# The second VectorE pass of an expert unit one gap later, alternating unit buffers, and a chunk loop written out

## The chip, the cores and the metric

One core of one Trainium2 chip. The metric is the device time of the whole launch in microseconds; smaller is better. TensorE does the matmuls, VectorE, ScalarE and GpSimd work on tiles in SBUF and (the first two) in PSUM, SyncE issues most transfers. Each engine runs its own list of instructions in order; they meet at semaphores.

## The reference

Input x of 32 sequences of 64 tokens of 128 features goes through four blocks, each added to its input:

```
x = x + recurrent_attention(layernorm(x), cond, ctx)   # 64 steps, one after the other
x = x + moe(layernorm(x))                              # 64 experts of width 64, top 8, plus a shared one
x = x + transformer_block(layernorm(x), cond, ctx)     # two attentions and a gated feed-forward
x = x + x @ weight.T + pooled(x) @ disha
```

The change touches the first two. A step of the recurrence computes logits = [x, h] @ W_attn.T + b, their softmax, the weighted sum over the context, comb = relu([x, applied] @ W_comb.T + b) and h = tanh(comb @ W_ih.T + h @ W_hh.T + b). The mixture of experts computes, for each expert, silu(x @ Wg) * (x @ Wu) * coef and multiplies it by Wd; all are summed.

## The kernel before

**Tiling.** The 64 steps of the recurrence are cut into 4 chunks (CH) of 16 steps (SPC). A chunk has 512 tokens (CT), which are the 512 columns of its tiles. As soon as a chunk has left the recurrence, its experts are computed, beside the recurrence of the next chunks. The experts go in pairs: 32 pairs (PAIRS) and the shared expert are 33 units (UNITS), numbered 0 to 32; unit 32 is the shared one.

**Stages and gaps.** All engines walk through the same plan, `stages` (line 455). Stage k runs the recurrence of chunk k, the norm, routing and first units of chunk m = k-1, and the last units of chunk k-2 (`tail`). Stages 0 and 1 are written out, stages 2 and 3 are a hardware loop (`Fori`, line 459), stages 4 and 5 have no recurrence. A stage has 64 gaps, four for each step of the recurrence (IDLE_GAPS); the place of a gap is its number modulo 4. The text calls four gaps of one step "a step", and counts them from 0 to 15 in a stage. In a gap an engine first does its operation of the recurrence and then what else the plan puts there. The order of the work on each engine is thus written by hand, and no engine goes past a wait.

**The recurrence by places** (function `rnn` of each engine). Place 0: TensorE makes the logits (lines 1451, 1452, 1462), VectorE the negative maximum `nmax` (1020), ScalarE the exp (765). Place 1: VectorE the reciprocal (1024) and `diag` (1026), TensorE eT (1465), VectorE `eb` in two parts (1030, 1034). Place 2: TensorE the 49 matmuls of comb (1469, 1475), VectorE `comb` (1038). Place 3: TensorE hn (1483, 1484), ScalarE the tanh `Hc` (771).

**A unit** n of chunk m, which begins at gap g = 28 + 2n of stage m+1 (units from gap 64 on run in the next stage, as `tail`):

- TensorE, gap g: six matmuls into PSUM bank n % 2 and bank 2 + n % 2 (line 1529).
- ScalarE, gap g: tanh into `th` (801). For n = 0 it copies the routing weights `coefT` before (796); SyncE stores them and loads them back, broadcast, as `coef_wide` (524, 533).
- VectorE, gap g+1: the first pass, `ga` = (th + 1) * bank (1168), and at once the second, `gu` = ga * other bank (1173).
- GpSimd, gap g+1: `hid` = gu * coef (637).
- TensorE, gap g+5: the down matmul into bank 5, over all units (1536).

So in gaps of odd number VectorE has both passes, and before them the operations of place 1 or 3. The buffers `th`, `gu`, `hid` and the banks are indexed by n % 2. As 33 is odd, unit 32 of a chunk and unit 0 of the next have the same buffers; `others` (line 448) gives the count up to which the users of a buffer must have come, and for n = 0 it is the whole chunk before. Units 31 and 32 both begin at gap 90, 26 of the next stage. Their sum is added to the residual by `add_units` (1175 to 1180) at gap END_GAP = 96, gap 32 of the next stage; the down matmul of unit 0 of the next chunk, which overwrites bank 5, waits for it (x2_ready, line 1534).

In the profile the tiles ga, gu and hid are named ex, th is thcb, coef_wide is xn, and PSUM is ps.

Of the kernel before, what the change touches and what calls it, by code (L numbers as in the profile page):

```python
# [8 lines left out]
ALU = mybir.AluOpType  # L9
ACT = mybir.ActivationFunctionType  # L10
# [6 lines left out]
WSCALE = 16.0  # L17
# [33 lines left out]
def build(nc, ins, out):  # L51
# [5 lines left out]
    CH = 4  # L57
# [3 lines left out]
    PAIRS = E // 2  # L61
# [11 lines left out]
    with ctx:  # L73
# [40 lines left out]
        wg = sb("wg", [P, PAIRS, 2, P], F16)  # L114
        wu = sb("wu", [P, PAIRS, 2, P], F16)
        wd = sb("wd", [P, PAIRS, P])
        swgu = sb("swgu", [P, 2, 2, P], F16)
        swd = sb("swd", [P, P])
# [81 lines left out]
        th = thcb[:, 0]  # L200
        ctx_tok = thcb[:, :, :, :].rearrange("p a b (n d) -> p (a b n) d", d=P)
        ga = ex[:, 2, :]
        gu = ex[:, 3:5, :]
        hid = ex[:, 5:7, :]
# [104 lines left out]
        def bank(i):  # L309
            return ps[:, i, :]  # L310
# [6 lines left out]
        def first(k):  # L317

            return isinstance(k, int) and k == 0
# [117 lines left out]
               **{gap: ("route", i) for i, gap in enumerate(g for g in range(10, 26) if g % IDLE_GAPS)}, 26: "coefT"}  # L437
        UNITS = PAIRS + 1
        U0 = 28
        unit_gap = [U0 + 2 * min(n, PAIRS - 1) for n in range(UNITS)]  # L440
        END_GAP = unit_gap[-1] + 6

        def units_at(gap, m, tail, delay=0):

            return [(chunk, n) for chunk, g in ((tail, gap + GAPS), (m, gap)) if chunk is not None
                    for n in range(UNITS) if unit_gap[n] + delay == g]

        def others(m, n):

            if isinstance(m, int) and m == 0 and n < 2:  # L450
                return None

            return m * UNITS + n - (1 if n else 0)

        def stages(eng, stage):

            stage(0, None, None, True)
            stage(1, 0, None, True)
            with eng.Fori(0, CH - 2) as j:
                stage(j + 2, j + 1, j, True)  # L460
            stage(CH, CH - 1, CH - 2, False)
            stage(CH + 1, None, CH - 1, False)

# [92 lines left out]
        def _(pool):  # L556
# [71 lines left out]
            def unit(m, n):  # L628
                done = m * UNITS + n
                pool.wait_ge(s["gu_ready"], done + 1)  # L630
                if n < PAIRS:
                    pool.wait_ge(s[f"coef_in{n // 2 % 2}"], 32 * (m * (PAIRS // 4) + n // 4 + 1))
                if others(m, n) is not None:
                    pool.wait_ge(s["y_ready"], others(m, n))
                wide = coef_wide[:, n // 2 % 2, n % 2 * CT:(n % 2 + 1) * CT]
                other = wide if n < PAIRS else k_shared.broadcast_to([P, CT])
                nc.gpsimd.tensor_tensor(hid[:, n % 2, :], gu[:, n % 2, :], other, ALU.mult)\  # L637
                  .then_inc(s["hid_ready"], 1)

            def stage(k, m, tail, recur):  # L640
# [66 lines left out]
            for n in range(ITEMS):  # L707
                k, g, a, j = item(n)
# [10 lines left out]
            with pool.Fori(0, CH // 2) as j:  # L719
                k = Tally(pool, s["f_pool"], 4)  # L720
# [11 lines left out]
        def _(act):  # L732
# [58 lines left out]
            def unit(m, n):  # L791
                if n == 0:
                    act.wait_ge(s["coefT_ps"], m + 1)
                    if not first(m):
                        act.wait_ge(s["coef_stored"], 16 * m)
                    nc.scalar.copy(coefT, bank(7)[0:E, :]).then_inc(s["coefT_ready"], 1)
                done = m * UNITS + n
                act.wait_ge(s["gu_ps"], done + 1)
                if others(m, n) is not None:
                    act.wait_ge(s["gu_ready"], others(m, n))  # L800
                nc.scalar.activation(th[:, n % 2, :], bank(n % 2), ACT.Tanh, scale=0.5 / WSCALE)\  # L801
                  .then_inc(s["th_ready"], 1)

            def stage(k, m, tail, recur):
# [84 lines left out]
            for n in range(-1, ITEMS + 1):  # L889
                k, j = divmod(n, 4)  # L890
# [39 lines left out]
        def _(dve):  # L930
            V = nc.vector
# [83 lines left out]
            def rnn(k, st, place):  # L1015
                t = k * SPC + st
                logits_bank, comb_bank, eT_bank, _ = (bank(i) for i in step_banks(k))
                if place == 0:
                    dve.wait_ge(s["logits_ready"], t + 1)
                    V.tensor_reduce(nmax[:, :], logits_bank[0:B, 0:L], AX_X, ALU.max, negate=True)\  # L1020
                     .then_inc(s["nmax_ready"], 1)
                elif place == 1:
                    dve.wait_ge(s["exp_ready"], t + 1)
                    rt.settle(V.reciprocal(rsum[:, :], esum[:, :]))

                    V.tensor_scalar(diag[:, :], ident[0:B, 0:B], rsum[:, :], 2.0, mul, mul)\  # L1026
                     .then_inc(s["diag_ready"], 1)
                    dve.wait_ge(s["eT_ready"], t + 1)

                    V.tensor_tensor(eb[:, 0, :], eT_bank[:, ET], ebmask[:, :], mul).then_inc(s["eb_hi"], 1)  # L1030
                    dve.wait_ge(s["eb_hi"], t + 1)
                    for a in range(2):
                        r = slice(a * L, (a + 1) * L)
                        V.tensor_tensor(eb[r, 1, a::2], eT_bank[r, ET][:, a::2], eb[r, 0, a::2], sub)\
                         .then_inc(s["eb_lo"], 1)
                elif place == 2:
                    dve.wait_ge(s["comb_ps_ready"], t + 1)
                    V.tensor_scalar(comb[:, :], comb_bank[:, COMB], bcomb[:, :], 0.0, add, ALU.max)\
                     .then_inc(s["comb_ready"], 1)
# [120 lines left out]
                                    csum[:, :].unsqueeze(2).unsqueeze(3).broadcast_to([P, TPC, PAIRS, 2]), mul)\  # L1160
                     .then_inc(s["coef_ready"], 1)

            def unit(m, n):
                done = m * UNITS + n
                dve.wait_ge(s["th_ready"], done + 1)
                if others(m, n) is not None or n == 1:
                    dve.wait_ge(s["gu_ready"], done)
                V.scalar_tensor_tensor(ga[:, :], th[:, n % 2, :], 1.0, bank(n % 2), add, mul)\  # L1168
                 .then_inc(s["unit_dve"], 1)
                dve.wait_ge(s["unit_dve"], done + 1)  # L1170
                if others(m, n) is not None:
                    dve.wait_ge(s["hid_ready"], others(m, n))
                V.tensor_tensor(gu[:, n % 2, :], ga[:, :], bank(2 + n % 2), mul).then_inc(s["gu_ready"], 1)  # L1173

            def add_units(m):
                dve.wait_ge(s["y_ready"], (m + 1) * UNITS)
# [5 lines left out]
            def stage(k, m, tail, recur):  # L1182
                if recur:
                    rt.round(k)
                if m is not None:
                    pt.round(m)
                for gap in gaps_of(m, tail):
                    st, place = divmod(gap, IDLE_GAPS)
                    if recur:
                        rnn(k, st, place)  # L1190
                    if first(k) and gap in SPLITS:
                        c = SPLITS[gap]
                        dve.wait_ge(s["weights_hi"], c + 1)
                        V.scalar_tensor_tensor(halves_of[c][1], landing_view(c), WSCALE, halves_of[c][0], mul, sub)\
                         .then_inc(s["weights_lo"], 1)
                    if first(k) and gap in LATE_OUT and setup_sem[LATE_OUT[gap]] == "setup_dve":
                        setup(LATE_OUT[gap])
                    if first(k) and gap in STOPS:
                        stops(STOPS[gap])
                    if m is not None and gap in PRO:  # L1200
                        part(m, PRO[gap])
                    if tail is not None and gap + GAPS == END_GAP:
                        add_units(tail)
                    for chunk, n in units_at(gap, m, tail, 1):
                        unit(chunk, n)

            stages(dve, stage)

# [200 lines left out]
        def _(pe):  # L1409
# [109 lines left out]
            def unit(m, n):  # L1519
                if n == 0:  # L1520
                    pe.wait_ge(s["xn2T_ready"], 2 * m + 2)
                    pe.wait_ge(s["weights_lo"], WEIGHTS)
                    pe.wait_ge(s["moe_w_in"], 16 * MOE_DMAS)
                if others(m, n) is not None:
                    pe.wait_ge(s["gu_ready"], others(m, n))
                for w, bk in ((wg, n % 2), (wu, 2 + n % 2)):
                    of = w[:, n] if n < PAIRS else swgu[:, bk // 2]
                    for i, (u, v) in enumerate(HALVES):
                        last = mm(bank(bk), of[:, u, :], xn2_half(m, v), start=(i == 0), stop=(i == 2))  # L1529
                last.then_inc(s["gu_ps"], 1)  # L1530

            def down(m, n):
                if n == 0 and not first(m):
                    pe.wait_ge(s["x2_ready"], m)
                pe.wait_ge(s["hid_ready"], m * UNITS + n + 1)
                mm(bank(5), wd[:, n, :] if n < PAIRS else swd[:, :], hid[:, n % 2, :],  # L1536
                   start=(n == 0), stop=(n == UNITS - 1)).then_inc(s["y_ready"], 1)

            def stage(k, m, tail, recur):
# [215 lines left out]
```

## Time and profile before

| | us |
|---|---|
| median of 3 runs | 1224.45 |
| lowest and highest | 1223.15, 1224.51 |
| profiled execution | 1223.28 |
| its span, first to last instruction | 1221.2 |
| TensorE matmuls busy | 1055.8 (86%) |
| VectorE busy | 742.1 (61%) |
| GpSimd busy | 512.8 (42%) |
| ScalarE busy | 429.8 (35%) |
| mean granted clock of TensorE | 0.864 of 2.4 GHz |

A timeline has one line for an instruction, or for a few alike: its start in us from the span's start, its time in us, the engine (PE is TensorE, PEld its weight loads, DVE VectorE, ACT ScalarE, POOL GpSimd), the line of the kernel, what it writes and reads, how many, and in brackets the idle time of the engine before it with what ended it. The time of an instruction includes what it waits for once it has started. The clock is 1.00 for 2.4 GHz and 0.50 for 1.2 GHz.

### The profile page before, as it was taken

To read this page: it belongs to the slowest core of one execution; us is meant where nothing else is said; L and a number is where in the kernel's file an instruction comes from. 1 tells how busy PE (TensorE), PEld (TensorE's weight loads), DVE (VectorE), ACT (ScalarE), POOL (GpSimd) and SP (SyncE) were. 2 spreads that over 40 slices of the span, in tenths; PEclk is the share of its full clock that TensorE was granted. 3 is DMA by queue.
4 is the path that set the end of the run, shared out by engine and by line. 5 is a ranking of instruction groups with operands and counts; after the bars stand their busy time and mean duration, and the time that the engine had idled before them with its cause. 6 is when DMAs were issued, how large, how long until landed. Compare 5 with 4: busy or idle time off the path is not lost. (4 is left out here: it accounts for less than half of the span.)

```text
span 1221.2 us, 31046 instructions
## 1 busy us (share of the span) xinstructions
PE 1055.8 (86%) x12668; PEld 701.2 (57%) x12668; DVE 742.1 (61%) x1882; ACT 429.8 (35%) x798; POOL 512.8 (42%) x452
## 2 busy tenths in 40 slices
PE   2699777789998999989997997799899999997867
PEld 2577655545555555545553443677677677775445
DVE  5544444445567554765569565678777678775553
ACT  1211011112221221212221222677778677775111
POOL 4788200003322332322333455576666666664010
PEclk9555555559999998889999999799999999999878
DMA  9020026012212221113222342000000000000000
GB/s 241 19 57 1 1 43 121 1 47 63 70 53 54 74 70 54 53 36 74 70 70 70 90 121 70 1 3 3 3 3 2 3 3 3 2 3 3 1 18 17
DMA packets 46066, 51.67 MB, mean 42 GB/s; under 512 B 22086, under 2 KB 36584, under 8 KB 45928
## 3 DMA queue, kind: packets, MB, share of 16 engines
q1 hardware_dynamic: 43010, 48.71, 15.7%
q8 instruction: 101, 1.65, 0.6%
q10 hardware_dynamic: 2918, 1.01, 0.5%
q14 instruction: 37, 0.30, 0.1%
HBM read 48.13 MB, written 1.57 MB: 41 GB/s over the span
## 5 line engine op out<-in xcount | busy, mean ns | idle before, releaser
L637 POOL TENSOR_TENSOR ex<-ex,xn 128x512 f32<-128x512 f32 x128 | 162.5, 1271 | 368.0 <-DVE ex L1173 275.3
L801 ACT ACTIVATE thcb<-ps 128x512 f32<-128x512 f32 x132 | 78.6, 596 | 283.1 <-PE ps L1529 283.1
L702 POOL TENSOR_TENSOR wu<-encC,wu 128x1024 f16<-128x1024 f32 x64 | 137.7, 2167 | 56.5 <-ACT encC L876 56.5
L1168 DVE SCALAR_TENSOR_TENSOR ex<-thcb,ps 128x512 f32<-128x512 f32 x132 | 90.6, 687 | 89.8 <-ACT thcb L801 87.1
L1536 PE MATMUL ps<-ex,wd 128*128 128x512 f32 x256 | 138.9, 625 | 1.9 <-POOL ex L637 1.9
L1529 PE MATMUL ps<-xnT,wg 128*128 (+1 forms) x384 | 109.3, 395 | 6.5 <-DVE ex L1173 6.4
L1529 PE MATMUL ps<-xnT,wu 128*128 (+1 forms) x384 | 109.7, 396 | 0.0
L1589 PE MATMUL ps<-wg,M 128*128 128x128 f16 x1536 | 98.2, 222 | 2.1 <-DVE wg L1262 2.1
L1589 PEld LDWEIGHTS ps<-wg,M 128*128 128x128 f16 x1536 | 93.1, 99 | 6.8 <-DVE wg L1262 2.5
L1173 DVE TENSOR_TENSOR ex<-ex,ps 128x512 f32<-128x512 f32 x132 | 90.7, 687 | 7.3 <-POOL ex L637 2.8
L696 POOL TENSOR_TENSOR wd<-wd,a_sum 128x512 f32<-128x512 f32 x64 | 66.5, 1042 | 65.7 <-DVE a_sum L1293 65.7
L1624 PE MATMUL ps<-N,wg 128*128 128x512 f16 x384 | 91.9, 381 | 0.6 <-DVE ex L1275 0.5
L869 ACT CAST wu<-ps 128x1024 f16<-128x1024 f32 x64 | 65.0, 1015 | 75.7 <-PE ps L1624 75.7
L1475 PEld LDWEIGHTS ps<-eb,encC 128*128 128x128 f16 x3072 | 91.1, 101 | 0.0
L1475 PE MATMUL ps<-eb,encC 128*128 128x2 f16 x3072 | 88.6, 164 | 0.0
L1284 DVE TENSOR_REDUCE a_max<-ps 128x8 bf16<-128x512 f32 x64 | 44.3, 692 | 48.6 <-PE ps L1604 48.3
L765 ACT ACTIVATE e_sb<-ps,nmax 32x128 f32<-32x128 f32 x64 | 22.9, 358 | 132.8 <-DVE nmax L1020 132.8
L1465 PE MATMUL ps<-diag,e_sb 32*128 32x32 f32 x128 | 31.2, 327 | 43.8 <-DVE diag L1026 43.8
L1529 PEld LDWEIGHTS ps<-xnT,wu 128*128 128x128 f16 x384 | 38.8, 101 | 49.3 <-issue 6.9
L876 ACT COPY encC<-ps 128x1024 f32<-128x1024 f32 x64 | 64.8, 1012 | 5.4
L1465 PEld LDWEIGHTS ps<-diag,e_sb 32*128 32x128 f32 x128 | 23.7, 229 | 71.7 <-DVE diag L1026 68.1
L1529 PEld LDWEIGHTS ps<-xnT,wg 128*128 128x128 f16 x384 | 31.4, 99 | 58.1 <-issue 30.2
(295 smaller groups left out, 1937.1 us busy)
## 6 DMA issues: line engine op xcount, KB each, us to landing
xn<-coef_rows SPq DMA_DIRECT2D x128, 256.0 KB, 3.8
thcb<-in_L_ffn_Wg SPq DMA_DIRECT2D x8, 256.0 KB, 3.8
thcb<-in_L_ffn_Wu SPq DMA_DIRECT2D x8, 256.0 KB, 3.1
wd<-in_L_ffn_Wd SPq DMA_DIRECT2D x2, 1024.0 KB, 11.4
xtok<-in_x SPq DMA_DIRECT2D x4, 256.0 KB, 6.0
thcb<-in_ctx SPq DMA_DIRECT2D x2, 512.0 KB, 11.1
wu<-in_L_xcond_attn_wq SPq DMA_DIRECT2D x2, 512.0 KB, 10.9
wu<-in_L_xcond_attn_wk SPq DMA_DIRECT2D x2, 512.0 KB, 10.6
```

The source lines that it names most:

```text
L637: nc.gpsimd.tensor_tensor(hid[:, n % 2, :], gu[:, n % 2, :], other, ALU.mult)\
L696: nc.gpsimd.tensor_tensor(half, half, a_sum[:, u, :].rearrange("p (m b) -> p m b", b=2).unsqueeze(3) .broadcast_to([P, 4, 2, 64]), ALU.mul ...
L702: nc.gpsimd.tensor_tensor(z[:, 1, 8 * u:8 * u + 8, :], a_Zc[:, u], z[:, 0, 8 * u:8 * u + 8, :], ALU.subtract)\
L801: nc.scalar.activation(th[:, n % 2, :], bank(n % 2), ACT.Tanh, scale=0.5 / WSCALE)\
L869: nc.scalar.copy(a_Z[:, n % 2, 0, 8 * u:8 * u + 8, :], ps[:, 2 * u:2 * u + 2, :].rearrange("p v (h d) -> p (v h) d", d=P)).then_inc(s["a_Z ...
L1168: V.scalar_tensor_tensor(ga[:, :], th[:, n % 2, :], 1.0, bank(n % 2), add, mul)\
L1173: V.tensor_tensor(gu[:, n % 2, :], ga[:, :], bank(2 + n % 2), mul).then_inc(s["gu_ready"], 1)
L1475: last = mm(comb_ps[:, 2 * j:2 * j + 2], encC[:, u, j, :], eb[:, v, 2 * j:2 * j + 2], start=False, stop=(v == 1 and j == NPAIR - 1))
L1529: last = mm(bank(bk), of[:, u, :], xn2_half(m, v), start=(i == 0), stop=(i == 2))
L1536: mm(bank(5), wd[:, n, :] if n < PAIRS else swd[:, :], hid[:, n % 2, :], start=(n == 0), stop=(n == UNITS - 1)).then_inc(s["y_ready"], 1)
L1589: m = mm(bank(b)[:, h * P:(h + 1) * P], M[a][:, u, 4 * b + h, :], a_h[:, k % 2, v, j * P:(j + 1) * P], start=(i == 0), stop=(i == 2))
L1624: m = mm(bank(2 * u + v), src[:, x, :], N[a][:, w, h:h + 4, :].rearrange("p h d -> p (h d)"), start=(i == 0), stop=(i == 2))
```

## The change

Three things. First, VectorE's `unit` is split: `gated` (first pass) stays in gap g+1, `product` (second pass) goes to gap g+2, right behind VectorE's operation of the recurrence in that gap, which for g+2 is that of place 0 or 2. Second, unit 32 begins at gap 91 in place of 90, END_GAP becomes 97, and `th`, `gu`, `hid` and the banks alternate by the running number of the unit over all chunks (`side`), so that each unit has other buffers than the one before; `others` is then the same formula for all units. Third, the hardware loop over stages 2 and 3 is written out.

```diff
-        unit_gap = [U0 + 2 * min(n, PAIRS - 1) for n in range(UNITS)]
+        unit_gap = [U0 + 2 * n - (n == PAIRS) for n in range(UNITS)]
         END_GAP = unit_gap[-1] + 6
...
-            if isinstance(m, int) and m == 0 and n < 2:
-                return None
-
-            return m * UNITS + n - (1 if n else 0)
+            done = m * UNITS + n
+            return done - 1 if done >= 2 else None
+
+        def side(m, n):
+
+            return (m * UNITS + n) % 2
...
-            with eng.Fori(0, CH - 2) as j:
-                stage(j + 2, j + 1, j, True)
+            for k in range(2, CH):
+                stage(k, k - 1, k - 2, True)
...
-            def unit(m, n):
+            def gated(m, n):
                 done = m * UNITS + n
                 dve.wait_ge(s["th_ready"], done + 1)
-                if others(m, n) is not None or n == 1:
+                if done:
                     dve.wait_ge(s["gu_ready"], done)
-                V.scalar_tensor_tensor(ga[:, :], th[:, n % 2, :], 1.0, bank(n % 2), add, mul)\
+                V.scalar_tensor_tensor(ga[:, :], th[:, side(m, n), :], 1.0, bank(side(m, n)), add, mul)\
                  .then_inc(s["unit_dve"], 1)
+
+            def product(m, n):
+                done = m * UNITS + n
                 dve.wait_ge(s["unit_dve"], done + 1)
                 if others(m, n) is not None:
                     dve.wait_ge(s["hid_ready"], others(m, n))
-                V.tensor_tensor(gu[:, n % 2, :], ga[:, :], bank(2 + n % 2), mul).then_inc(s["gu_ready"], 1)
+                V.tensor_tensor(gu[:, side(m, n), :], ga[:, :], bank(2 + side(m, n)), mul).then_inc(s["gu_ready"], 1)
...
                     if recur:
                         rnn(k, st, place)
+                    for chunk, n in units_at(gap, m, tail, 2):
+                        product(chunk, n)
...
                     for chunk, n in units_at(gap, m, tail, 1):
-                        unit(chunk, n)
+                        gated(chunk, n)
```

The other lines of the diff put `side(m, n)` in the place of `n % 2` on GpSimd, ScalarE and TensorE.

## Rows read from the trace of the kernel before

**Rows 1.** The page: its head, and TensorE's granted clock in 40 slices.

```profile
span 1221.2 us, 31046 instructions
...
PEclk9555555559999998889999999799999999999878
```

**Rows 2.** Windows: stretch, its length, busy us (instructions) of each engine, clock, DMA.

```profile
449.03:456.77 7.74, 7.74 (x79) 4.35 (x78) 4.13 (x11) 1.82 (x7) 2.53 (x2) 1.00 0.24 70
332.49:343.86 11.37, 11.21 (x95) 6.62 (x94) 5.87 (x20) 2.33 (x8) 2.10 (x2) 1.00 0.17 48
472.24:489.53 17.29, 15.67 (x95) 9.01 (x94) 6.07 (x21) 2.44 (x8) 2.29 (x2) 0.70 0.12 33
```

**Rows 3.** Timeline of a steady step: start, us, engine, line, out<-in [idle before].

```profile
449.88 0.69 DVE L1173 TENSOR_TENSOR ex<-ex,ps 128x512 f32<-128x512 f32 x1
...
450.64 1.27 POOL L637 TENSOR_TENSOR ex<-ex,xn 128x512 f32<-128x512 f32 x1 [2.42 <-DVE ex L1173]
...
450.83 0.21 DVE L1020 TENSOR_REDUCE nmax<-ps 32x1 f32<-32x64 f32 x1 [0.27 <-PE ps L1462]
...
451.39 0.81 PE L1529 MATMUL ps<-xnT,wu 128*128 x3
451.56 0.15 DVE L1024 RECIPROCAL rsum<-esum 32x1 f32<-32x1 f32 x1 [0.52 <-ACT e_sb L765]
451.75 0.23 DVE L1026 TENSOR_SCALAR diag<-ident,rsum 32x32 f32<-32x32 f32 x1
...
452.13 0.29 PEld L1465 LDWEIGHTS ps<-diag,e_sb 32*128 32x128 f32 x2 [0.42 <-DVE diag L1026]
```

**Rows 4.** Line 1026 in 280 to 330 and in 580 to 622: ns least/median/most.

```profile
L1026 DVE TENSOR_SCALAR diag<-ident,rsum x7: 228/228/230, 281.1 to 327.5; 32x32 f32<-32x32 f32 x7
...
L1026 DVE TENSOR_SCALAR diag<-ident,rsum x6: 228/228/231, 581.6 to 620.3; 32x32 f32<-32x32 f32 x6
```

**Rows 5.** Timeline of a step that is late on VectorE.

```profile
364.11 0.69 DVE L1173 TENSOR_TENSOR ex<-ex,ps 128x512 f32<-128x512 f32 x1
...
364.71 0.20 DVE L1020 TENSOR_REDUCE nmax<-ps 32x1 f32<-32x64 f32 x1
...
365.62 0.55 DVE L1026 TENSOR_SCALAR diag<-ident,rsum 32x32 f32<-32x32 f32 x1
...
366.22 0.40 PE L1465 MATMUL ps<-diag,e_sb 32*128 32x32 f32 x2 [1.24 <-DVE diag L1026]
```

**Rows 6.** Timeline at 82.9 and at 92.4, VectorE and GpSimd starting together.

```profile
82.95 1.30 DVE L1026 TENSOR_SCALAR diag<-ident,rsum 32x32 f32<-32x32 f32 x1
82.96 1.26 POOL L618 TENSOR_TENSOR cen<-xn,ex 128x512 f32 x1 [0.19 <-POOL ex L616]
...
92.45 0.23 DVE L1026 TENSOR_SCALAR diag<-ident,rsum 32x32 f32<-32x32 f32 x1
92.53 1.28 POOL L616 TENSOR_TENSOR ex<-ex 128x512 f32<-128x512 f32 x1 [0.19 <-POOL ex L616]
```

**Rows 7.** Timeline of gaps 32 and 33 of stage 2.

```profile
410.86 2.49 POOL L637 TENSOR_TENSOR ex<-ex,xn 128x512 f32<-128x512 f32 x2 [4.63 <-DMA xn<-coef_rows]
410.89 0.21 DVE L1020 TENSOR_REDUCE nmax<-ps 32x1 f32<-32x64 f32 x1 [1.13 <-PE ps L1462]
411.08 1.22 DVE L1179 TENSOR_TENSOR xT<-xT,ps 128x512 f32 x1
...
413.44 0.40 PE L1465 MATMUL ps<-diag,e_sb 32*128 32x32 f32 x2 [1.18 <-DVE diag L1026]
```

**Rows 8.** The loop's line on TensorE's queue, and the first logits behind it.

```profile
L459 PEldq COMPARE_BRANCH  x2: 83/1802/3521, 470.8 to 623.9; - x2
...
474.63 0.40 PE L1451 MATMUL ps<-w_attnT,xnc 128*32 128x128 f32 x2 [1.62 <-issue]
```

**Rows 9.** Timeline: three matmuls of a unit at the lower clock.

```profile
482.98 1.49 PE L1529 MATMUL ps<-xnT,wu 128*128 x3
```

**Rows 10.** Timeline: the last down of the last chunk.

```profile
755.24 1.13 PE L1536 MATMUL ps<-ex,swd 128*128 128x512 f32 x2
```

More of the change, by code:

```diff
@@ L636, in unit @@
                 other = wide if n < PAIRS else k_shared.broadcast_to([P, CT])
-                nc.gpsimd.tensor_tensor(hid[:, n % 2, :], gu[:, n % 2, :], other, ALU.mult)\
+                nc.gpsimd.tensor_tensor(hid[:, side(m, n), :], gu[:, side(m, n), :], other, ALU.mult)\
                   .then_inc(s["hid_ready"], 1)
@@ L800, in unit @@
                     act.wait_ge(s["gu_ready"], others(m, n))
-                nc.scalar.activation(th[:, n % 2, :], bank(n % 2), ACT.Tanh, scale=0.5 / WSCALE)\
+                nc.scalar.activation(th[:, side(m, n), :], bank(side(m, n)), ACT.Tanh, scale=0.5 / WSCALE)\
                   .then_inc(s["th_ready"], 1)
@@ L1525, in unit @@
                     pe.wait_ge(s["gu_ready"], others(m, n))
-                for w, bk in ((wg, n % 2), (wu, 2 + n % 2)):
+                for w, bk in ((wg, side(m, n)), (wu, 2 + side(m, n))):
                     of = w[:, n] if n < PAIRS else swgu[:, bk // 2]
@@ L1535, in down @@
                 pe.wait_ge(s["hid_ready"], m * UNITS + n + 1)
-                mm(bank(5), wd[:, n, :] if n < PAIRS else swd[:, :], hid[:, n % 2, :],
+                mm(bank(5), wd[:, n, :] if n < PAIRS else swd[:, :], hid[:, side(m, n), :],
                    start=(n == 0), stop=(n == UNITS - 1)).then_inc(s["y_ready"], 1)
```

## The prediction

> **What bounds the kernel now.** I read the page first, for the span of 1221.2 us [rows 1]. The run it comes from took 1223.28 us, so 2.1 us lie around the span; the median of the three runs shown is 1224.45. All sums below start from 1223.28. The change touches only the part from the first unit (step 7 of stage 1) to the last `add_units`, about 262 to 757 us. Then I cut this part into steps of four gaps, which a tanh of the recurrence (line 771) marks. A step that has two units and nothing else takes 7.74 us, with TensorE busy all 7.74 [rows 2]. So TensorE, in order, is the bound there, and whatever makes it wait adds in full.
>
> Where could it be made to wait? Within the step the recurrence is a chain: logits, maximum (line 1020), exp, reciprocal (1024), diag (1026), eT on TensorE (1465). TensorE covers the chain with one unit's six matmuls [rows 3]. The reader should see two things. `product` (line 1173) ends at 450.57, but the maximum waits for TensorE's logits until 450.83: in such a step the second pass delays the maximum by nothing, and its old place is empty time. And diag ends at 451.98, with TensorE at eT from 452.13: that chain has 0.1 us to spare. Steps like this one, with diag at 0.23 us and eT about 0.15 behind it, are 24 in all: 7 in stage 1, 8 in stage 2, 9 in stage 3 [rows 4] (the first seven and the last six).
>
> Ten further steps, early in stages 2 and 3, are late on VectorE, which has routing work: there the maximum does come behind `product`, and TensorE stands still before eT, 1.24 us in the one shown [rows 5]; these pauses run from 0.2 to 1.9 us.
>
> **The port.** diag takes 0.23 us alone. Where GpSimd runs it takes 0.55 and ends at 366.17 [rows 5], while the GpSimd operation started right behind `product`, at 0.07 after its end. Two pairs show who wins [rows 6]. At 82.95 diag starts 0.01 us before a GpSimd operation, yet lasts 1.30 and ends 0.03 behind it. At 92.45 GpSimd starts 0.08 us behind it and diag takes 0.23. So diag loses unless it leads by more than 0.01, and surely wins from 0.08 on; when it loses it waits to GpSimd's end plus 0.03.
>
> **Part 1, the second pass behind the recurrence's operation.** For even gaps of place 0, `product` now stands between the maximum and the reciprocal. Worked out on the steady step [rows 3], with the maximum unchanged at 450.83: the next operation of VectorE starts 0.19 later (410.89 to 411.08) [rows 7], so `product` runs 451.02 to 451.71. GpSimd's multiply starts 0.07 to 0.08 behind it (450.57 to 450.64) [rows 3], at 451.79, and ends 1.27 later, 453.06. The reciprocal can start 0.09 before `product` ends (364.80 to 364.71) [rows 5], at 451.62, which is behind exp's 451.56; diag 0.19 later, at 451.81. GpSimd is first by 0.02, where it has been seen to win even 0.01 late. So diag ends at 453.09 and eT starts 0.05 later (366.17 to 366.22) [rows 5]: 453.14 in place of 452.13, **+1.01 us** per step. Bounds: +0.0 if diag gets in first (it would end at 452.04, within TensorE's own time), and +1.1 if the 0.1 spare is not there. TensorE has nothing to put in the gap, as its queue is in order. 24 steps: **+24.2**. Step 7 of stage 2, where eT had 0.35 behind diag: +0.8. There, TensorE's unit 0 also has to wait for `product` of unit 31, now behind the maximum in the same gap (line 1525's wait), for 0.9 us; this falls into the same pause and costs nothing more while diag stalls.
>
> Late steps: the maximum comes up to 0.72 earlier, since the pass no longer precedes it, but diag then ends 2.25 behind the maximum (0.19 + 0.69 + 0.07 + 1.27 + 0.03) in place of 1.46. Six steps, whose logits are ready over 0.72 before: +0.08 each. Four, whose maximum is late by 0.03 to 0.21 only: +0.5 to +0.74, together 2.7. Sum **+3.1**.
>
> At place 2 `product` goes behind comb (line 1038). comb feeds hn, which stands behind six matmuls on TensorE: nobody waits, only two pauses of 0.22 could go. Taken as 0. The consumers have room: down(n) comes five gaps behind unit n, and unit n+2 four.
>
> The Trainium skill, page SBUF — State Buffer, section SBUF: two separate sides, calls the pair of ports that VectorE and GpSimd share an exclusive lock: whichever starts first has it for the whole instruction. By its letter diag should have won at 82.95; there it lost, so I go by the rows [rows 6]. It speaks against this change just the same: with GpSimd 0.02 us first, it gives +1.0 too, and with diag first the rival below.
>
> **Part 2, unit 32 in gap 27, END_GAP 97.** `add_units` moves to gap 33, where down(0) waits for it. In step 8 of stages 2 and 3, before: maximum, add of 1.22, diag behind two GpSimd operations, pause of 1.18, eT at 413.44 [rows 7]. After: diag slips in behind the first GpSimd operation (eT about 412.2), then eb (1.0), add (1.2), and only then down(0), about 414.6 in place of 413.8: +0.8 each, up to 2.0 if diag has to wait for both. I take 0.8, since the diag that waited at 82.95 ended 0.03 behind one GpSimd operation, though more were queued [rows 6]: **+1.6**. Without the recurrence, unit 32 stands behind one more down, 1.0 to 1.1 us [rows 10]: the copy of coefT in stage 4, on which the loads depend that bind there, comes 1.1 later, and the very end about 0.8 later: **+1.9**. The alternating buffers take away the wait of unit 0 for unit 32, worth 0.1 in stage 2 and nothing in stage 4, where those loads bind.
>
> **Part 3, the loop written out.** TensorE's branch back takes 3.52 us, and TensorE is idle 1.62 us before the logits [rows 8]. The step takes 17.29 us at a clock of 0.70, the same step of stage 2 11.37 at 1.00 [rows 2]. Without the branch I take all of it, **-5.9**; the other end is -1.4, the idle time alone, if the clock falls anyway. Code in a straight line was fetched unseen everywhere else, so its length costs 0. The row only says "issue"; that a taken branch forces a fetch of its target is what the Trainium skill says (Runtime: NRT & Kernel Launch, section Instruction fetch mechanics).
>
> **The clock.** Of nine pauses of TensorE over 1 us in stages 2 and 3, four were followed by a stretch at 1.2 GHz in place of 2.4; the page shows it as 8 in slices 16 to 18 (458 to 550 us) [rows 1]. Three matmuls take 1.49 there against 0.81 [rows 3, 9], so a unit costs 1.3 more. The change makes 25 new pauses of about 1 us and lengthens four. They are shorter than the ones that did it, so I take a quarter: 6 or 7 falls by 1.4 us, **+9**. Bounds 0 and +20 (half of them).
>
> **The sum.** 24.2 + 0.8 + 3.1 + 1.6 + 1.9 - 5.9 + 9 = +34.7, so 1223.3 + 34.7 = **1258 us**, +2.8%.
>
> **Rivals.**
> (A) The same, and the clock holds: 1249 us. For it: in stage 2 five pauses of 1.2 to 1.9 us left the clock alone. Chance 0.22.
> (B) diag wins the race, and the change is faster. Place: lines 1024 to 1026 behind `product`. It needs GpSimd 0.03 to 0.10 us later against diag than the rows say. Then the 24 steps cost 0, the six late ones gain 0.96 each (diag ends 1.21 behind a maximum 0.72 earlier), the four others 0.2 to 0.43, together -7.0; with +1.6, +1.9 and -5.9: 1214 us. Against it: all intervals used repeat to 0.01 us from step to step. Chance 0.12.
> (C) The move does not do what it says, because some steps stall and others not, or the written-out loop gives more than its idle time and clock show: 1225 to 1240. Chance 0.06.
> (D) Forecast, stalls and some half clock: 1252 to 1275. Chance 0.60.
>
> **How the numbers follow.** The likeliest case gives 1258. The range 1236 to 1273 holds D but for its top, A, and half of C: about 0.8. What a measurement can tell from no change is about 0.2%, 2.4 us. Faster is B: 0.12. Same 0.02. Slower is the rest: 0.86.
>
> **What would show it.** Right: diag (line 1026) at about 1.3 us in most steps, ending 0.03 behind line 637; a steady step of 8.75 us; TensorE idle 1.0 before line 1465; no long branch near 471 us; step 0 of stage 3 near 11.4 us. Wrong: diag at 0.23 with line 637 starting behind it, and steps of 7.74. If the clock's page row shows more than slices 16 to 18 below 9, the time goes towards 1273 or over.

## The result, and the profile after

The changed kernel takes **1279.71 us** (median of 4 runs, 1274.23 to 1282.30) against 1223.80 for the kernel before (4 runs): ratio **1.0454**, 95% interval 1.0415 to 1.0492. It is slower, as predicted, but by 56 us, not by 35, and outside the range of 1236 to 1273. The profiled execution took 1278.36 us, with a span of 1276.6.

The page of the changed kernel: its head, and TensorE's granted clock in 40 slices. It answers to [rows 1].

```profile
span 1276.6 us, 30526 instructions
...
PEclk9555555579898988988889899899999999999878
```

Before, only slices 16 to 18 of 10 to 25 stood below 9. Now nine of the slices 11 to 23 do. By windows over the whole part in question, from the end of step 7 of stage 1 to the end of the recurrence (stretch, length, busy us (instructions) of TensorE, its weight loads, VectorE, ScalarE and GpSimd, clock, DMA share, GB/s), first the kernel before, then the changed one:

```profile
268.95:625.27 356.32, 341.18 (x3215) 192.06 (x3216) 208.88 (x620) 78.72 (x211) 107.30 (x87) 0.95 0.23 62
```

```profile
269.19:677.58 408.39, 371.58 (x3215) 206.54 (x3216) 232.72 (x621) 81.16 (x211) 106.91 (x87) 0.88 0.20 54
```

This pair splits the loss in two. The stretch is 52.1 us longer. The same 3215 matmuls are busy for 30.4 us more (the clock, 0.88 in place of 0.95), and TensorE is idle for 21.7 us more (36.8 less 15.1). What TensorE waited for in the same stretch (sum in us, times, longest), before and after:

```profile
PE ps L1465 <- DVE diag L1026: 12.5, 12, 1.9
```

```profile
PE ps L1472 <- DVE diag L1028: 30.7, 33, 1.8
PE ps L1543 <- DVE xT L1184: 3.8, 2, 1.9
PE ps L1536 <- DVE ex L1178: 2.0, 2, 1.0
```

So diag is the wait that was turned on, 33 times in place of 12. The second line is `add_units`, behind which down(0) stands in step 8. The third is unit 0, which in step 7 of stages 2 and 3 waits for `product` of unit 31.

A steady step of the changed kernel as a timeline, which answers to [rows 3]:

```profile
289.30 0.21 DVE L1022 TENSOR_REDUCE nmax<-ps 32x1 f32<-32x64 f32 x1 [0.99 <-PE ps L1469]
289.44 0.67 DVE L1178 TENSOR_TENSOR ex<-ex,ps 128x512 f32<-128x512 f32 x1
...
290.03 0.15 DVE L1026 RECIPROCAL rsum<-esum 32x1 f32<-32x1 f32 x1
290.18 1.26 POOL L639 TENSOR_TENSOR ex<-ex,xn 128x512 f32<-128x512 f32 x1 [2.04 <-DVE ex L1178]
290.21 1.26 DVE L1028 TENSOR_SCALAR diag<-ident,rsum 32x32 f32<-32x32 f32 x1
...
291.53 0.40 PE L1472 MATMUL ps<-diag,e_sb 32*128 32x32 f32 x2 [0.87 <-DVE diag L1028]
```

GpSimd starts 0.03 us ahead of diag, diag lasts 1.26 in place of 0.23 and ends 0.03 behind GpSimd, and eT follows 0.06 later. diag ends 2.17 behind the maximum's start; the prediction had 2.25. Step 7 of stage 2 shows that not every VectorE operation is held up in this way:

```profile
419.91 1.27 POOL L639 TENSOR_TENSOR ex<-ex,xn 128x512 f32<-128x512 f32 x1 [6.17 <-DVE ex L1178]
419.94 0.69 DVE L1170 SCALAR_TENSOR_TENSOR ex<-thcb,ps 128x512 f32<-128x512 f32 x1
419.98 0.81 PE L1536 MATMUL ps<-xnT,wg 128*128 128x512 f16 x3 [0.99 <-DVE ex L1178]
...
420.72 0.49 DVE L1028 TENSOR_SCALAR diag<-ident,rsum 32x32 f32<-32x32 f32 x1
```

The first pass, which reads one operand from SBUF and one from PSUM, starts 0.03 us behind GpSimd and still takes its usual 0.69. The reciprocal, with one operand in SBUF, isn't held either (0.14 us at 420.54). diag, which reads `ident` and `rsum`, both in SBUF, is held until 0.03 behind GpSimd. By windows, two steady steps of stage 1, two of stage 2, and step 0 of stage 3 ([rows 2] has the like of before):

```profile
278.81:287.48 8.67, 7.80 (x79) 4.35 (x78) 5.00 (x11) 1.82 (x6) 2.24 (x3) 1.00 0.22 61
287.48:296.16 8.68, 7.81 (x79) 4.35 (x78) 4.91 (x11) 1.82 (x6) 2.81 (x3) 1.00 0.26 62
489.81:500.07 10.26, 9.39 (x79) 5.08 (x79) 4.89 (x12) 1.94 (x5) 2.52 (x2) 0.83 0.22 53
500.07:510.32 10.25, 9.38 (x79) 5.07 (x79) 4.90 (x12) 1.93 (x5) 2.52 (x2) 0.83 0.19 52
510.32:521.53 11.21, 11.21 (x95) 6.78 (x95) 6.73 (x20) 2.34 (x7) 2.15 (x2) 1.00 0.19 48
```

At full clock the steady step is 8.67 to 8.68 us (predicted 8.75). But the same step is 10.25 where the clock is 0.83, that is, where TensorE spends a third of the step at 1.2 GHz: 79 matmuls are busy for 9.38 us, not 7.81. Of the 24 steady steps, 18 hold such a stretch (here and below: over half a microsecond of the step at 1.2 GHz). A unit's three matmuls in the step of 500.07 show both levels, one after the other in the same step:

```profile
502.57 0.81 PE L1536 MATMUL ps<-xnT,wu 128*128 128x512 f16 x3
...
508.14 1.49 PE L1536 MATMUL ps<-xnT,wu 128*128 128x512 f16 x3
```

**Where the 55.4 us of span went** (to within rounding), by the steps of the two traces (each step from tanh to tanh):

| part | predicted | measured |
|---|---|---|
| pauses in 24 steady steps | +24.2 | +22.6 (24 x 0.94) |
| clock in these steps | +9 (for all steps) | +29.0 |
| ten late steps | +3.1 | +2.9 |
| step 7 of stage 2 | +0.8 | +0.8 |
| step 8, stages 2 and 3 | +1.6 | +2.5 |
| step 0 of stage 3 (loop) | -5.9 | -6.1 |
| behind the recurrence | +1.9 | +3.1 |
| rest | 0 | +0.5 |

The 24 steps went from 186.1 to 239.0 us. Of these 52.9, 22.6 are pauses, 1.3 is unit 32's matmuls, which step 7 of stage 3 took over from step 6, and 29.0 is left, the clock: 18 steps at 9.9 to 10.5 in place of 8.68. The late steps are 0.3 longer as they stand, and 2.9 with the 2 x 1.3 us put back that went from their last to step 7. Of the 24 steps, step 7 of stage 3 is the one whose pause, 0.99 us, is the wait of unit 0 and not that of eT.

### The profile page after: what moved, and what is told of

It is laid out like the page before. It is cut to its first block and busy times, and to the rows that moved or that the text cites. A ratio compares the mean times of both kernels' runs of the same rounds, so it can differ in the third digit from the quotient of the medians.

```text
span 1276.6 us, 30526 instructions
## 1 busy us (share of the span) xinstructions
PE 1087.3 (85%) x12668; PEld 716.7 (56%) x12668; DVE 765.6 (60%) x1882; ACT 432.3 (34%) x798; POOL 511.8 (40%) x452
## 3 DMA queue, kind: packets, MB, share of 16 engines
q10 hardware_dynamic: 2918, 1.01, 0.4%
## 5 line engine op out<-in xcount | busy, mean ns | idle before, releaser
L1543 PE MATMUL ps<-ex,wd 128*128 128x512 f32 x256 | 142.1, 637 | 7.9 <-POOL ex L639 4.1
L1536 PE MATMUL ps<-xnT,wg 128*128 128x512 f16 x384 | 121.2, 431 | 7.0 <-DVE ex L1178 7.0
L1536 PE MATMUL ps<-xnT,wu 128*128 128x512 f16 x384 | 123.0, 436 | 0.0
L1536 PEld LDWEIGHTS ps<-xnT,wu 128*128 128x128 f16 x384 | 42.1, 110 | 58.9 <-issue 23.9
## 6 DMA issues: line engine op xcount, KB each, us to landing
wd<-in_L_ffn_Wd SPq DMA_DIRECT2D x2, 1024.0 KB, 10.5
wu<-in_L_xcond_attn_wk SPq DMA_DIRECT2D x2, 512.0 KB, 10.7
```

## Experiments

All ratios are to the kernel before on the same chip; times are medians. Diffs are against the changed kernel unless the text says otherwise.

**1. u_loop: the kernel before, with its loop written out.**

```diff
-            with eng.Fori(0, CH - 2) as j:
-                stage(j + 2, j + 1, j, True)
+            for k in range(2, CH):
+                stage(k, k - 1, k - 2, True)
```

> The kernel before with nothing changed but the loop over stages 2 and 3 written out. Theory: the branch back of TensorE (3.5 us) and the half clock behind it go, so step 0 of stage 3 falls from 17.3 to about 11.4 us and the whole by 6: about 1218 us (1216 to 1220), steady steps stay at 7.74 us and diag (line 1026 of before) at 0.23. Rival, that the longer code costs something in fetching or shifts the clock for the worse: 1223 us or more, with idle time before no named wait.

Measured: 1220.45 us (10 runs, 1215.37 to 1225.24), ratio 0.9991 (0.9954 to 1.0028): no gain to be seen. Step 0 of stage 3, by windows:

```profile
476.72:491.05 14.33, 14.26 (x95) 8.10 (x94) 6.33 (x23) 2.33 (x7) 2.71 (x3) 0.76 0.13 38
```

The branch's idle time is gone (14.26 busy of 14.33), yet the clock is 0.76, and the step takes 14.33, not 11.4. The step gives 3.0 us of the forecast 5.9, 1.6 of them the idle time; the rest of its loss at the lower clock (0.70 in [rows 2]) did not hang on the branch. In the time of the whole kernel even the 3.0 can't be told from nothing. Nor does the full gain of the step show there: in experiment 9, also with the loop written out, this step takes 11.20 us at clock 1.00, and the ratio is 1.0009. The ten late steps spend 27.3 us at 1.2 GHz there, against 13.6 in the kernel before.

**2. u_side: everything but the move.** `product` goes back into gap g+1.

```diff
-                    for chunk, n in units_at(gap, m, tail, 2):
-                        product(chunk, n)
...
                         gated(chunk, n)
+                        product(chunk, n)
```

> The changed kernel with the second pass back in gap g+1, right behind the first: written-out loop, unit 32 in gap 27, END_GAP 97 and alternating buffers stay. Theory (port, then clock): these parts cost 1.5 to 5 us over the written-out loop alone, by the later sum (down of unit 0 waits for it) and the later unit 32: about 1221 us (1218 to 1225), steady steps 7.74 us, diag 0.23 us, no new half clock. Rival, that the buffers or unit 32 bring the half clock: over 1240 us with the second pass at its old place.

Measured: 1231.11 us (9 runs), ratio 1.0096 (1.0061 to 1.0132). Steady steps are back at 7.74 us with diag at 0.23, so the move alone makes the stall. But what is left costs 12 us (0.0096 of 1221.7, the kernel before on that chip), and 10.7 more than experiment 1, where the expectation was far lower. One place is step 7, in a timeline:

```profile
407.12 0.21 DVE L1022 TENSOR_REDUCE nmax<-ps 32x1 f32<-32x64 f32 x1 [2.34 <-PE ps L1468]
407.26 0.66 DVE L1170 SCALAR_TENSOR_TENSOR ex<-thcb,ps 128x512 f32<-128x512 f32 x1
...
407.95 0.69 DVE L1178 TENSOR_TENSOR ex<-ex,ps 128x512 f32<-128x512 f32 x1
408.56 0.14 DVE L1026 RECIPROCAL rsum<-esum 32x1 f32<-32x1 f32 x1
```

Unit 32 now begins in an odd gap, so its passes fall in a gap of place 0, and both stand between the maximum and the reciprocal. The prediction had costed the later `add_units` and one more down, and overlooked this. TensorE stands still for 0.54 us before eT. That pause explains little of the whole by itself: steps 7 and 8 of both stages together take 44.8 us against 35.9 in experiment 1, and of these 8.9, 2.6 are unit 32's matmuls, which stood in step 6, 1.1 are the two pauses, and most of the rest is step 8 at a mean clock of 0.81 and 0.78 (1.00 in experiment 1).

**3. x_hold: GpSimd made to wait for diag.** Where `product` stands at place 0, GpSimd's multiply waits for diag. (`held` gives the count of that step's diag, and None for the other units.)

```diff
+                if held(m, n) is not None:
+                    pool.wait_ge(s["diag_ready"], held(m, n))
                 pool.wait_ge(s["gu_ready"], done + 1)
```

> The changed kernel, but GpSimd's multiply of the units whose second pass stands behind the maximum waits for diag of the same step, so diag is always first at the port; VectorE's order is that of the changed kernel. Port theory: diag takes 0.23 us again and ends about 1.15 to 1.2 behind the maximum's start, a steady step is 7.74 to 7.8 us at full clock, the six late steps gain almost 1 us each: 1210 to 1220 us, faster than both kernels. Rival (VectorE's own time: the pass of 0.67 us between maximum and reciprocal is what delays diag): steady steps stay at 8.3 us or more and the whole over 1250 us.

Measured: **1210.27 us** (10 runs, 1205.78 to 1216.71), ratio 0.9926 (0.9890 to 0.9961). Timeline and window of a steady step:

```profile
430.01 0.21 DVE L1028 TENSOR_REDUCE nmax<-ps 32x1 f32<-32x64 f32 x1 [0.99 <-PE ps L1475]
430.16 0.66 DVE L1184 TENSOR_TENSOR ex<-ex,ps 128x512 f32<-128x512 f32 x1
...
430.93 0.23 DVE L1034 TENSOR_SCALAR diag<-ident,rsum 32x32 f32<-32x32 f32 x1
431.24 1.27 POOL L645 TENSOR_TENSOR ex<-ex,xn 128x512 f32<-128x512 f32 x1 [2.65 <-DVE diag L1034]
```

```profile
428.20:435.94 7.74, 7.74 (x79) 4.35 (x78) 3.88 (x11) 1.83 (x7) 2.54 (x3) 1.00 0.25 71
```

One wait on GpSimd turns +4.5% into -0.7%. `product` still stands ahead of the reciprocal, yet diag ends 1.15 behind the maximum's start, not 2.17: VectorE's own time there costs nothing, and all of diag's delay comes from GpSimd. None of the 24 steady steps holds a stretch at 1.2 GHz. This is also rival B brought about by hand, and the gains it named are there: TensorE's idle time in the ten late steps is 3.75 us against 10.40 before, 6.65 less, where B had 7.0. On the prediction's base of 1223.28 the ratio makes 1214 us, which is B's time.

Steps 7 of both stages still take 10.08 us, although diag takes 0.23 there and eT doesn't wait. 1.3 us are unit 32's matmuls, and 0.99 is a pause earlier in the step: unit 0 waits for `product` of unit 31. The prediction named this wait, at 0.9, and expected it to cost nothing more as long as diag stalls.

**4. x_fill: four idle matmuls ahead of TensorE's wait for diag**, in steps with units.

```diff
                 elif place == 1:
+                    if chunk >= 2 or chunk == 1 and st >= 8:
+                        for i in range(4):
+                            mm(bank(4), wg[:, 0, 0, :], xn2_half(0, 0), start=True, stop=True)
                     pe.wait_ge(s["diag_ready"], t + 1)
```

> The changed kernel with four extra matmuls of 512 columns into the unused bank 4 just before TensorE waits for diag, in every step that has units (about 0.86 us of work in a pause of 0.87; the result is not used). Clock theory: the work fills the pause, the clock stays at 2.4 GHz, a steady step is 8.7 us in place of 10.25, diag still takes 1.26 us: 1243 to 1253 us, faster with more work. Rival (the half clock does not come from the pauses): steady steps stay at 10.2 us or get longer by the extra work, 1280 us or more.

Measured: 1254.68 us (4 runs), ratio 1.0275 (1.0215 to 1.0335), 22 to 25 us (by ratios, by medians) less than the changed kernel although it does more. Step 9 of stage 1 and step 10 of stage 2, by windows:

```profile
279.85:288.54 8.69, 8.67 (x83) 4.74 (x82) 5.01 (x11) 1.83 (x7) 2.27 (x3) 1.00 0.19 61
...
444.01:452.70 8.69, 8.68 (x83) 4.74 (x82) 4.92 (x11) 1.83 (x6) 2.54 (x3) 1.00 0.23 62
```

The stall is untouched (diag 1.27 us, step 8.69), TensorE is idle for 0.01 to 0.02 us in place of 0.87, and the clock holds in all 24 steady steps but one. This separates the two losses of a steady step: the stall is the 0.94, the clock the rest. The 24 steps give back 27.2 us, more than the kernel does, since other steps lose: the two steps 8 take 14.0 and 13.7 us at clock 0.77 and 0.78, and step 0 of stage 3 takes 15.2 at 0.78.

**5. x_half: GpSimd multiplies 256 of the 512 columns.** The other half of `hid` is left out.

```diff
-                nc.gpsimd.tensor_tensor(hid[:, side(m, n), :], gu[:, side(m, n), :], other, ALU.mult)\
+                nc.gpsimd.tensor_tensor(hid[:, side(m, n), 0:256], gu[:, side(m, n), 0:256], other[:, 0:256], ALU.mult)\
```

> The changed kernel with GpSimd's multiply cut to 256 of the 512 columns (half of hid is left out, so the output is not the reference's). Port theory: the multiply takes 0.65 us, diag waits for it and ends at about 1.56 us behind the maximum's start in place of 2.18, TensorE's pause falls from 0.87 to 0.25 us and a full-clock steady step is 8.05 us (7.99 to 8.1). If the shorter pause still brings a half-clock stretch in a step now and then, the whole is 1235 to 1260 us; if not, about 1232. Rival (VectorE's own pass): diag's end does not depend on GpSimd's size, a full-clock step stays at 8.68.

Measured: 1230.45 us (10 runs), ratio 1.0067 (1.0036 to 1.0098). The time is 1.6 us under the "about 1232" that was expected if the clock holds, though it fell now and then, for which 1235 to 1260 stood. The steady step, timeline and window:

```profile
441.83 0.72 POOL L639 TENSOR_TENSOR ex<-ex,xn 128x256 f32<-128x256 f32 x1 [2.86 <-DVE ex L1178]
441.86 0.73 DVE L1028 TENSOR_SCALAR diag<-ident,rsum 32x32 f32<-32x32 f32 x1
```

```profile
439.13:447.27 8.14, 7.81 (x79) 4.35 (x78) 4.37 (x11) 1.82 (x6) 1.45 (x2) 1.00 0.25 66
```

diag shrinks with GpSimd's operation, from 1.26 to 0.73 for 1.26 to 0.72. TensorE's pause is 0.33. Its step is 0.40 longer than 7.74, and 21 of the 24 steps hold the clock (one of the 21 has 0.50 us at 1.2 GHz).

**6 and 7. x_place0 and x_place2: only the passes of one place moved.** In x_place0 `product` goes one gap later only where that gap is of place 0, in x_place2 only where it is not.

```diff
                     for chunk, n in units_at(gap, m, tail, 2):
-                        product(chunk, n)
+                        if (gap % IDLE_GAPS == 0):
+                            product(chunk, n)
...
                         gated(chunk, n)
+                        if not ((gap + 1) % IDLE_GAPS == 0):
+                            product(chunk, n)
```

> The changed kernel with only every second second pass moved: those that stand behind the maximum (place 0); the others are back in gap g+1. Theory (port, then clock): all of the harm is here, diag 1.26 us, steady steps 8.68 to 10.25 us, the whole 1270 to 1285 us. Rival (moving a pass behind any operation of the recurrence costs alike): about half, 1255 us.

> The counterpart: only the second passes behind comb (place 2) are moved, those at the maximum are back in gap g+1. Theory: no cost in steady steps (7.74 us, diag 0.23 us), so the same as the version with no pass moved (1231 us), 1225 to 1234. Rival: half of the loss, 1255 us.

Measured: x_place0 1285.58 us (one run, so without an interval), x_place2 1229.38 us (10 runs), ratio 1.0074 (1.0041 to 1.0107). The passes of place 0 carry the whole loss: with them alone 21 steady steps hold a stretch at 1.2 GHz. With those of place 2 alone 22 of the 24 steady steps take 7.74 to 7.9 us, and the time is that of experiment 2 within its interval. The prediction's 0 for place 2 holds.

**8. x_best: experiment 3, with units 31 and 32 both at gap 90 as before**, END_GAP 96, and for these two both passes in one gap.

```diff
-        unit_gap = [U0 + 2 * n - (n == PAIRS) for n in range(UNITS)]
+        unit_gap = [U0 + 2 * min(n, PAIRS - 1) for n in range(UNITS)]
```

> As the version where GpSimd waits for diag (1210 us), but units 31 and 32 are back in gap 90 with END_GAP 96, and the two have both passes in one gap, as before; the buffers still alternate. Theory: steps 7 and 8 of stages 2 and 3 give back what the later unit 32 and the later sum cost (10.1 and 10.7 to 12.1 us in that version, 7.9 and 9.9 before), and the last two stages 1 to 3 us: 1200 to 1208 us. Rival (these steps are bound by the loads of the coefficients and the later sum is hidden behind them): 1208 to 1212, no better.

Measured: **1205.20 us** (6 runs, 1201.89 to 1207.78), ratio 0.9863 (0.9819 to 0.9908): faster than both kernels. Steps 7 and 8 of stage 2 by windows:

```profile
397.89:405.63 7.74, 7.74 (x79) 4.34 (x78) 4.30 (x12) 2.29 (x7) 2.31 (x2) 1.00 0.16 48
405.64:415.25 9.61, 8.66 (x81) 4.73 (x80) 4.98 (x12) 1.82 (x7) 3.42 (x3) 1.00 0.54 134
```

In experiment 3 they took 10.08 and 12.11, 1.3 of it unit 32's matmuls. With the passes of units 31 and 32 in one gap unit 0 no longer waits in step 7 (0.99 less), and with END_GAP 96 TensorE's pause in step 8 falls from 1.91 to 0.95.

**9. u_alt: experiment 2 with unit 32 back at gap 90** (the diff of experiment 8): written-out loop and alternating buffers, nothing else.

> The kernel before with the loop written out and the buffers alternating over all units, but units 31 and 32 both at gap 90 and END_GAP 96 as before, and both passes in one gap. Theory: the alternation costs nothing, and what the kernel with unit 32 at gap 91 lost against the one with the loop alone (1231.1 against 1220.5) came from unit 32's new gap. Then 1216 to 1224 here, with step 7 of stages 2 and 3 at 7.7 to 7.9 us. Rival: the alternation itself costs (another wait, or another place of the half clock), and 1227 to 1233 comes out with step 7 still near 7.9.

Measured: 1222.27 us (10 runs), ratio 1.0009 (0.9983 to 1.0034). Step 7 is 7.74 us in both stages. The theory stands: alternation costs nothing that can be measured, and the 9 to 11 us between this kernel and experiment 2 (by medians, by ratios) are unit 32's new gap, with END_GAP behind it. The two were put back together, so what each is worth stays open.

**10. x_unit32: the changed kernel with unit 32 back at gap 90**, both passes of units 31 and 32 in one gap.

> The changed kernel, but units 31 and 32 begin in gap 90, their passes stand in one gap, and END_GAP is 96. Theory: the late place of unit 32 costs step 7 about 2.3 us (10.08 to 7.8) and the end 1 to 2 us, while the stalls and the half clock of the other steps stay: 1268 to 1275. Rival: the clock takes it back, since the steps of 10.08 us stood at full clock and the saved time is lost to half clock in another step: 1277 to 1284.

Measured: 1276.17 us (4 runs, 1271.35 to 1279.58), ratio 1.0449 (1.0389 to 1.0508), between the two expectations and no different from the changed kernel's 1.0454. The profile shows the rival at work. Steps 7 of both stages fall from 10.08 to 7.74 us, step 8 of stage 2 from 11.84 to 9.89. But in stage 1, steps 9 to 13 now take 10.0 to 10.2 us; in the changed kernel they took 8.68. All but one of the 24 steady steps hold a stretch at the lower clock. Steps 7 and 8 give 8.4 us in all; 2.6 go back to step 6 with unit 32's matmuls, and 5.8 would be left. In the two profiled executions the span is 1.2 us longer all the same, so other steps lose about 7, most of it (6.4) in the steady steps, to the clock. Why the clock held for those five steps in one kernel and not in the other stays open; steps 7 and 8 of stage 1 differ by 1.4 and 0.2 us there.

**11. x_fill2: two idle matmuls in place of four.**

> The changed kernel with two idle matmuls of 512 columns (0.43 us at full clock), in place of four, ahead of TensorE's wait for diag, in the steps with units. diag still stalls to 1.27 us and a steady step still needs at least 8.68; TensorE's idle time before eT falls from 0.87 to about 0.44. Theory A, the length of the pause decides: at 0.33 (GpSimd's multiply halved) the clock held in the steady steps, so at 0.44 it holds too, steps stay at 8.68 with clock 1.00, and 1252 to 1262 comes out. Theory B, what decides is that the step of 8.68 us holds any pause at all: half clock stays in nearly every step, 10.25 us each, and 1274 to 1284 comes out.

Measured: 1263.87 us (4 runs), ratio 1.0353 (1.0296 to 1.0411), 2 us over theory A's range and far from B's. Windows of steps 9 and 11 of stage 1 and 10 of stage 2:

```profile
280.18:288.87 8.69, 8.24 (x81) 4.54 (x80) 5.01 (x11) 1.83 (x6) 2.27 (x3) 1.00 0.23 61
...
298.93:309.38 10.45, 10.00 (x81) 5.43 (x82) 4.91 (x12) 1.93 (x6) 2.53 (x2) 0.83 0.18 52
455.02:463.70 8.68, 8.24 (x81) 4.54 (x80) 4.91 (x11) 1.82 (x6) 2.53 (x3) 1.00 0.21 60
```

With a pause of 0.44 us per step, 18 of the 24 steps hold the clock and 6 don't. Both answers occur with the same pause, so its length shifts how often the clock falls and does not decide each step.

## Why the prediction came out as it did

**The port, Part 1: right, in mechanism and size.** The race was costed at GpSimd 0.02 us ahead; it is 0.03 ahead. Where it wins, diag ends 0.03 behind it. The step at full clock is 8.68, not 8.75: the maximum-to-`product` distance was taken from a pair with `add_units` (0.19) and is 0.14 here. 24 x 0.94 against 24 x 1.01. Rival B fell on the chip as the prediction's rows said, and experiment 3 shows that it was the right rival to fear: 65 to 69 us (by ratios, by medians) lie between the two outcomes, and GpSimd was first by 0.03 us.

**The clock: the term that failed.** The prediction took "a quarter" of 25 new pauses, since they were shorter than the four that had been followed by a fall, and +9 us. Three quarters of the steady steps fell instead, 18 of 24, at 1.6 us each (1.4 was assumed): +29. Even the upper bound of +20 did not hold it, as it assumed half of them. The error was to count pauses one by one, each against a pause of before. A pause of 0.87 us in step after step did what pauses of 1.2 to 1.9 us had not done in stage 2 of the kernel before. (The prediction counted five of these in stage 2; the trace has four there, and the fifth in stage 3.) The experiments show the cause. With the pause filled by four matmuls (experiment 4) 0.01 us is left and 1 of 24 steps falls, with half of GpSimd's operation (5) it is 0.33 us and 3, with two matmuls (11) 0.44 us and 6. Rival A, that the clock holds, named 1249 us; experiment 4, where it holds in the steady steps with the fillers included, measured 1254.68. The sign that the prediction gave for its own top end, more slices below 9 on the clock's page row, did come.

**Part 2: right where it was priced, with some clock on top.** The sum said +1.6 for the two steps 8 and +1.9 for the end. Steps 8 cost +2.5: TensorE's idle time in them went from 2.5 to 3.8 us, +1.3, by the wait for the later sum that was named, and the rest is the clock. The end cost +3.1, about half of it clock (10.2 us at 1.2 GHz behind the recurrence against 6.8). What was missed shows only with `product` at its old place: in experiment 2 both passes of unit 32 stand between maximum and reciprocal, a pause of 0.54 us in each step 7. Step 7 of stage 2 came out at the +0.8 of the sum by another wait. It was priced as diag's stall, with unit 0's wait for `product` of unit 31 inside it. In the trace that wait of 0.99 comes first and covers diag's, and in experiment 3, where diag doesn't stall, it stays. With the later sum it is what experiment 8 wins back: 5 to 8 us (medians, ratios).

**Part 3: the number right, its reason not.** Step 0 of stage 3 gained 6.1 us (11.21 at clock 1.00, predicted 11.4), but experiment 1 shows that the written-out loop doesn't secure it: 14.33 us there, and no gain in the time. Experiment 9 has the step at 11.20 and no gain in the time either. The other end of that term, -1.4, is nearer to what the edit gives by itself. The sum was wrong by 20 us in one direction and lucky by up to 4.7 here.

**The late steps** came out at +2.9 for +3.1, and that is luck. The prediction's +3.1 were pauses. Steps 1 and 2 lost 0.5 and 0.7 in stage 2, as forecast (+0.5 to +0.74 each). In the other six the maximum was taken to come 0.72 earlier. Behind the logits it came 0.1 earlier in step 3, 1.2 in step 5 and 1.7 in step 6, so TensorE's pause before eT grew from 1.24 to 1.83 us in step 3 and fell from 1.3 and 1.87 to 0.87 in the other two. Together TensorE is idle for 10.6 us in the ten steps, against 10.4 before. The remaining 2.7 are the clock, which the sum had in another term: 20.5 us at 1.2 GHz, against 13.6.

## What to carry to other kernels

A short VectorE operation on the critical chain that reads its operands from SBUF, as diag does, must not be ready just behind the start of a long GpSimd operation. Its price here was GpSimd's whole duration, and the order was settled by hundredths of a microsecond, so it should be settled by a wait and not by timing. When an edit puts a pause on TensorE into every step of a steady loop, cost the step at both clock levels and take a stretch at the lower level as at least as likely as none (here 18 to 23 of 24 steps); scattered pauses were no guide to regular ones. And where a planned operation changes from an odd to an even gap, read what is now between the links of the chain in that gap, at the edges of the loop too.

## What the hardware showed beyond that

- The clock answers to pauses of TensorE that are well under a microsecond if they come in each step. Steady steps with a stretch at 1.2 GHz, of 24, by the pause before eT: with no pause 0 to 2 (none in the kernel before and in experiments 3, 8 and 9, one in 1 and 7, two in 2), 1 at 0.01 (4), 3 at 0.33 (5), 6 at 0.44 (11), 18, 21 and 23 at 0.87 (the changed kernel, 6 and 10). Which steps fall is not decided by the pause alone.
- Idle matmuls in a pause can pay: with four, 1.0 us of TensorE work per step took 22 to 25 us (ratios, medians) off a kernel bound by TensorE.
- diag waits for exactly GpSimd's operation: 1.26 us against 1.26, and 0.73 against 0.72 for half the columns, whatever its own 0.23 us. The Trainium skill (SBUF — State Buffer, section SBUF: two separate sides) says that the one which comes second blocks fully until the first ends; with GpSimd 0.03 us first, the traces agree. A pass that reads one operand from PSUM was not held (0.69 us at 419.94, with GpSimd at 419.91).
- A saving in a step at full clock can be lost to the clock elsewhere: about 7 us in the profiled pair of experiment 10, and the written-out loop's gain in experiments 1 and 9.
